# Norms of three tiles gathered in the tail, one sum moved to GpSimd, mixing by pairs, banks turned

## The reference

```python
zxbcdt = u @ in_proj_w.T                       # 512 -> 2 * 1024 + 2 * 128 + 64
z, xBC, dt_raw = jnp.split(zxbcdt, ...)
xBC = silu(causal_conv(xBC, 4 taps) + conv_b)
x, B, C = jnp.split(xBC, ...)
dt = softplus(dt_raw + dt_bias); A = -exp(A_log)
# in chunks of 64 tokens, 64 heads of 16 channels:
Y_diag = einsum(C, B, exp(differences of cumsum(dt * A)), x * dt)
state  = state * exp(sum(dt * A)) + einsum(B, decay to the chunk's end, x * dt)
Y_off  = einsum(C, state before the chunk, exp(cumsum(dt * A)))
y  = Y_diag + Y_off + x * D
yg = y * silu(z)
out = (yg * rsqrt(mean(yg ** 2) + eps) * norm_weight) @ out_proj_w.T
x1 = layernorm(u + out)
h  = silu(x1 @ w_gate.T) * (x1 @ w_up.T);  v = h @ w_down.T
result = layernorm(x1 + v / sqrt(mean(v ** 2) + eps))
```

## Time and profile before

| | us |
|---|---|
| median of 3 runs | 1842.28 |
| lowest and highest | 1840.56, 1845.46 |
| profiled execution, its own time | 1848.83 |
| span of the profiled execution | 1847.0 |
| PE busy | 1653.4 (90%) |
| DVE busy | 1382.8 (75%) |
| POOL busy | 1001.1 (54%) |
| ACT busy | 933.0 (51%) |

### The profile page before, as it was taken

How to read it: one execution, slowest core, us unless ns; L and a number is a source line. 1 busy time by engine, 2 the same in 40 slices (tenths; PEclk the granted TensorE clock), 3 DMA queues, 4 the chain that set the end, 5 groups by cost and what they waited for, 6 DMA issues and landing times. The chain is left out here.

```text
span 1847.0 us, 36975 instructions
## 1 busy us (share of the span) xinstructions
PE 1653.4 (90%) x11168; PEld 830.2 (45%) x11168; DVE 1382.8 (75%) x2200; ACT 933.0 (51%) x1647; POOL 1001.1 (54%) x1031
## 2 busy tenths in 40 slices
PE   2698999989989889888998898787999999999998
PEld 1244445444544444444544454454344444444443
DVE  6849858958867976985895896784777777777775
ACT  3454264444535335436444443432866666666662
POOL 0036526626625643652662663583877776767773
PEclk9899999999999999999999999898999999999999
DMA  6111131132124014113113212822001111101011
GB/s 220 50 39 28 49 86 49 28 79 69 29 54 102 16 55 104 28 49 83 51 30 75 72 29 54 228 47 62 35 23 47 57 35 47 57 35 52 29 35 58
DMA packets 214679, 109.66 MB, mean 59 GB/s; under 512 B 133796, under 2 KB 185696, under 8 KB 214496
## 3 DMA queue, kind: packets, MB, share of 16 engines
q1 hardware_dynamic: 214496, 107.37, 21.7%
HBM read 80.57 MB, written 26.76 MB: 58 GB/s over the span
## 5 line engine op out<-in xcount | busy, mean ns | idle before, releaser
L772 PE MATMUL ps_in<-u_hi,w_hi 128*128 128x512 f16 (+1 forms) x608 | 240.4, 395 | 80.4 <-DVE u_lo L1259 32.3
L1077 ACT ACTIVATE decay<-ps_d 128x512 f32<-128x512 f32 x256 | 149.8, 592 | 273.4 <-PE ps_d L830 222.3
L794 PE MATMUL ps_in<-w_out,zg 128*128 128x512 f32 x512 | 245.8, 636 | 32.9 <-DVE pre L1272 32.9
L1359 DVE TENSOR_TENSOR mix<-decay,gb 128x512 f32<-128x512 f32 x256 | 238.3, 938 | 47.7 <-issue 14.0
L1665 POOL TENSOR_TENSOR xend<-xpad,decay 128x256 f32<-128x256 f32 x256 | 186.9, 748 | 125.5 <-PE ps_yo L865 89.4
L772 PE MATMUL ps_in<-u_lo,w_hi 128*128 128x512 f16 (+1 forms) x608 | 238.6, 392 | 0.0
L772 PE MATMUL ps_in<-u_hi,w_lo 128*128 128x512 f16 (+1 forms) x608 | 237.6, 391 | 0.0
L1272 DVE SCALAR_TENSOR_TENSOR pre<-ps_in,cws,pre 128x511 f32<-128x511 f32 (+2 forms) x240 | 179.0, 746 | 34.1 <-ACT pre L1016 28.3
L1758 POOL TENSOR_TENSOR gate_sum<-gate_sum,gate_part 128x512 f32<-128x512 f32 x88 | 142.3, 1617 | 102.5 <-DVE gate_part L1586 102.3
L794 PEld LDWEIGHTS ps_in<-w_out,zg 128*128 128x128 f32 x512 | 101.2, 203 | 174.2 <-issue 172.3
L1016 ACT ACTIVATE pre<-ps_in,cb,cws 128x512 f32<-128x512 f32 x80 | 62.3, 779 | 181.2 <-PE ps_in L772 181.1
(11 more groups left out here) (181 smaller groups left out, 3743.3 us busy)
## 6 DMA issues: line engine op xcount, KB each, us to landing
ebc<-e_dram SPq DMA_DIRECT2D x256, 64.0 KB, 2.6
u<-u_t SPq DMA_DIRECT2D x9, 1024.0 KB, 5.0
res<-u_tok SPq DMA_DIRECT2D x32, 256.0 KB, 2.7
x_dram<-res SPq DMA_DIRECT2D x32, 256.0 KB, 2.0
xa<-x_dram SPq DMA_DIRECT2D x8, 1024.0 KB, 5.7
xr<-x_dram SPq DMA_DIRECT2D x32, 256.0 KB, 2.6
out<-xr SPq DMA_DIRECT2D x32, 256.0 KB, 2.0
fw_words<-gu_words SPq DMA_DIRECT2D x32, 176.0 KB, 3.1
```

Source lines behind the costliest of these rows:

```text
L772: last = mm(ps_in[bk][0:m, :], w[:, k, col:col + m], u[:, k, :], start=(k == 0 and j == 0), stop=(k == KT - 1 and j == 2))
L794: last = mm(ps_in[bk][:, :], zg[:, k, tt * P:(tt + 1) * P], w_out[:, k, :], start=(k == 0), stop=(k == CT - 1))
L1077: ac(decay[:, n % NG, :, :].rearrange("p a b -> p (a b)"), ps_d[n % 2][:, :], ACT.Exp).then_inc(e_done, 1)
L1359: v.tensor_tensor(mix[:, n % NG, :, :], decay[:, n % NG, :, :], gb[:, c % 2, 0:CH].unsqueeze(1).broadcast_to([P, CT, CH]), ALU.mult).then_ ...
```

## The change

- `banks_of` turns the two banks round behind q2: from x6 on, every use has the bank that it did not have before. x6 has the bank of q2, x7 that of o2, and so on.
- `res`, `bn`, `mv`, `rstd` and the semaphores `res_in` and `x1_out` have four places, one for each tile, where they had two. SyncE loads all four tiles of the residual at the start of a stage and stores all four at its end.
- `norm_tile` is split: `take_out` (forming `res`, which frees the bank) stays three slots after the projection; the statistics and the scaling of tiles 0 to 2 go to the tail, ahead of tile 3. GpSimd's second roots go with them, behind `sum_squares` of the last chunk and ahead of `root` of tile 3.
- The addition of `yoff` to `y` goes from VectorE (`y_before`) to GpSimd (`add_before`), at g = 3, ahead of `sum_squares`.
- `mixing` covers two slots with one instruction of 1024 columns, issued at every odd slot for the two slots that follow; `m_done` counts pairs.

```diff
 def banks_of(uses):
-    return [i % 2 for i in range(len(uses))]
+    names = [name for _, name in uses]
+    turned = names.index("q2") + 1 if "q2" in names else len(uses)
+    return [(i + (i >= turned)) % 2 for i in range(len(uses))]
...
-        res = sb("res", [P, 2, DM])
+        res = sb("res", [P, TT, DM])
...
             def body(st):
                 b = st.scan
-                load_res(b, 0)
-                load_res(b, 1)
+                for tt in range(TT):
+                    load_res(b, tt)
...
-                    for tt in range(2):
-                        if f"o{tt}" in st.at(n - NORM_END - 1):
-                            store_x1(b, tt)
-                            load_res(b, tt + 2)
-                store_x1(b, 2)
-                store_x1(b, 3)
+                for tt in range(TT):
+                    store_x1(b, tt)
...
             def within(b, n):
                 c, g = n // NG, n % NG
-                pe.wait_ge(m_done, b * SLOTS + n + 1)
+                pe.wait_ge(m_done, b * (SLOTS // 2) + n // 2 + 1)
...
             def exp_group(b, n):
                 act.wait_ge(d_full, b * SLOTS + n + 1)
-                need(act, m_done, b * SLOTS + n - 3)
+                need(act, m_done, b * (SLOTS // 2) + n // 2 - 1)
...
             def mixing(b, n):
-                dve.wait_ge(e_done, b * SLOTS + n + 1)
-                if n % NG == 0:
+                c, g = n // NG, n % NG
+                dve.wait_ge(e_done, b * SLOTS + n + 2)
+                if g == 0:
                     dve.wait_ge(t_free, (b * NC + c) * NA + 2)
-                need(dve, yd_done, b * SLOTS + n - 3)
-                v.tensor_tensor(mix[:, n % NG, :, :], decay[:, n % NG, :, :],
-                                gb[:, c % 2, 0:CH].unsqueeze(1).broadcast_to([P, CT, CH]), ALU.mult).then_inc(m_done, 1)
+                need(dve, yd_done, b * SLOTS + n - 2)
+                v.tensor_tensor(mix[:, g:g + 2, :, :].rearrange("p g e t -> p (g e) t"),
+                                decay[:, g:g + 2, :, :].rearrange("p g e t -> p (g e) t"),
+                                gb[:, c % 2, 0:CH].unsqueeze(1).broadcast_to([P, 2 * CT, CH]), ALU.mult).then_inc(m_done, 1)
...
             def y_before(b, c):
...
-                    dve.wait_ge(y1_done, b * 7 + c)
-                    dve.wait_ge(xd_done, b * NC + c + 1)
-                    v.tensor_tensor(y[:, c % 2, :, :], y[:, c % 2, :, :], yoff[:, :, :], ALU.add).then_inc(y2_done, 1)
...
-                    if n + 2 < SLOTS:
-                        mixing(b, n + 2)
+                    if n % 2 == 1 and n + 1 < SLOTS:
+                        mixing(b, n + 1)
...
                         if f"o{tt}" in st.at(n - NORM_AT):
-                            norm_tile(st, tt)
-                        if f"o{tt}" in st.at(n - NORM_END):
-                            norm_tile_end(st, tt)
+                            take_out(st, tt)
...
                 use_in(st, SLOTS, "x")
-                norm_tile_end(st, TT - 2)
+                for tt in range(TT - 1):
+                    norm_tile(st, tt)
+                for tt in range(TT - 1):
+                    norm_tile_end(st, tt)
                 use_in(st, SLOTS, "o")
...
+            def add_before(b, c):
+                pool.wait_ge(y1_done, b * 7 + c)
+                pool.wait_ge(xd_done, b * NC + c + 1)
+                g_.tensor_tensor(y[:, c % 2, :, :], y[:, c % 2, :, :], yoff[:, :, :], ALU.add).then_inc(y2_done, 1)
...
                     if g == 3 and c > 0:
+                        add_before(b, c)
                         sum_squares(b, c - 1)
...
-                        if f"o{tt}" in st.at(n - NORM_AT - 1):
-                            ln_root(b, tt)
                 gate(st, NC - 1)
-                ln_root(b, TT - 2)
                 sum_squares(b, NC - 1)
+                for tt in range(TT - 1):
+                    ln_root(b, tt)
                 root(st, TT - 1)
                 ln_root(b, TT - 1)
```

More of the change, by code:

```diff
@@ L65 @@
 SPLIT_SLOT = {1: (0, 1), 2: (2, 3)}
-NORM_AT, NORM_END = 3, 9
+NORM_AT = 3
 DEC = 352
@@ L285, in build @@
         rinv = sb("rinv", [P, TT])
-        bn = sb("bn", [P, 2, 6])
-        mv = sb("mv", [P, 2, 2])
-        rstd = sb("rstd", [P, 2])
+        bn = sb("bn", [P, TT, 6])
+        mv = sb("mv", [P, TT, 2])
+        rstd = sb("rstd", [P, TT])
         wmax = sb("wmax", [P, 2 * KT])
@@ L366, in build @@
         u_in = sem("u_in")
-        res_in = [sem("res_in0"), sem("res_in1")]
+        res_in = [sem(f"res_in{tt}") for tt in range(TT)]
         rq_in = [sem("rq_in0"), sem("rq_in1")]
@@ L374, in build @@
         parts_out = sem("parts_out")
-        x1_out = [sem("x1_out0"), sem("x1_out1")]
+        x1_out = [sem(f"x1_out{tt}") for tt in range(TT)]
         fw_in = [sem("fw_in0"), sem("fw_in1")]
@@ L559, in load_res @@
             def load_res(b, tt):
-                need(sp, x1_out[tt % 2], b * 32 + 16 * (tt // 2))
+                need(sp, x1_out[tt], b * 16)
                 settled(sp)
-                sp.dma_start(res[:, tt % 2, :], u_tok[bass.ds(b * L + tt * P, P), :]).then_inc(res_in[tt % 2], 16)
+                sp.dma_start(res[:, tt, :], u_tok[bass.ds(b * L + tt * P, P), :]).then_inc(res_in[tt], 16)
             def store_x1(b, tt):
@@ L567, in store_x1 @@
                 settled(sp)
-                sp.dma_start(x1_dram[bass.ds(b * L + tt * P, P), :], res[:, tt % 2, :]).then_inc(x1_out[tt % 2], 16)
+                sp.dma_start(x1_dram[bass.ds(b * L + tt * P, P), :], res[:, tt, :]).then_inc(x1_out[tt], 16)
             def load_fw(b, k):
@@ L648, in ahead @@
                 if n == 2 + W_STEPS:
-                    for k in range(2):
-                        sp.wait_ge(x1_out[k], 32)
+                    for tt in range(TT):
+                        sp.wait_ge(x1_out[tt], 16)
                     load_xa(0)
@@ L718, in _ @@
             body(Stage("last", nb - 1))
-            for k in range(2):
-                sp.wait_ge(x1_out[k], nb * 32)
+            for tt in range(TT):
+                sp.wait_ge(x1_out[tt], nb * 16)
             def load_xr(f, tt):
@@ L1060, in aux @@
                 else:
-                    need(act, m_done, b * SLOTS + NG * (c - 1))
+                    need(act, m_done, b * (SLOTS // 2) + 2 * (c - 1))
                     need(act, s_full, b * 14 + 2 * max(c - 1, 0))
@@ L1216, in ffn @@
                         if p.first and m == 1:
-                            for k in range(2):
-                                act.wait_ge(x1_out[k], nb * 32)
+                            for tt in range(TT):
+                                act.wait_ge(x1_out[tt], nb * 16)
                         silu(p, m)
@@ L1405, in mean_square, with take_out, norm_tile @@
                 v.tensor_scalar(msv[:, tt:tt + 1], src[:, 0:1], 1.0 / DI, 1e-5, ALU.mult, ALU.add).then_inc(free, 1)
-            def norm_tile(st, tt):
+            def take_out(st, tt):
                 b = st.scan
                 bk, _, full = st.bank(f"o{tt}")
-                i = tt % 2
-                ch = Chain(dve, ln_chain, 12, b)
-                ch.k = 3 * tt
                 dve.wait_ge(in_full[bk], full)
                 dve.wait_ge(rinv_done, b * TT + tt + 1)
-                dve.wait_ge(res_in[i], b * 32 + 16 * (tt // 2) + 16)
-                v.scalar_tensor_tensor(res[:, i, :], ps_in[bk][:, :], rinv[:, tt:tt + 1], res[:, i, :],
+                dve.wait_ge(res_in[tt], b * 16 + 16)
+                v.scalar_tensor_tensor(res[:, tt, :], ps_in[bk][:, :], rinv[:, tt:tt + 1], res[:, tt, :],
                                        ALU.mult, ALU.add).then_inc(in_free[bk], 1)
+            def norm_tile(st, tt):
+                bk, _, full = st.bank(f"o{tt}")
+                ch = Chain(dve, ln_chain, 12, st.scan)
+                ch.k = 3 * tt
                 dve.wait_ge(in_free[bk], full)
-                ch.step(v.bn_stats(bn[:, i, :], res[:, i, :]), settled)
-                ch.step(v.bn_aggr(mv[:, i, :], bn[:, i, :]))
-                v.tensor_scalar(mv[:, i, 1:2], mv[:, i, 1:2], 1e-5, None, ALU.add).then_inc(ln_chain, 1)
+                ch.step(v.bn_stats(bn[:, tt, :], res[:, tt, :]), settled)
+                ch.step(v.bn_aggr(mv[:, tt, :], bn[:, tt, :]))
+                v.tensor_scalar(mv[:, tt, 1:2], mv[:, tt, 1:2], 1e-5, None, ALU.add).then_inc(ln_chain, 1)
             def norm_tile_end(st, tt):
-                b, i = st.scan, tt % 2
-                dve.wait_ge(rstd_done, b * TT + tt + 1)
-                v.tensor_scalar(res[:, i, :], res[:, i, :], mv[:, i, 0:1], rstd[:, i:i + 1],
+                dve.wait_ge(rstd_done, st.scan * TT + tt + 1)
+                v.tensor_scalar(res[:, tt, :], res[:, tt, :], mv[:, tt, 0:1], rstd[:, tt:tt + 1],
                                 ALU.subtract, ALU.mult).then_inc(x1_done, 1)
@@ L1451, in body @@
                 mixing(b, 0)
-                mixing(b, 1)
                 for n in range(SLOTS):
@@ L1710, in ln_root @@
```

(2 more changed lines are left out.)

3 lines of the change are left out of this document (2 added, 1 removed).

## The result

The changed kernel takes 1782.78 us (median of 4 runs, 1782.3 to 1782.92). The kernel before, run beside it, took 1842.61 (median of 4 runs). The ratio is 0.9665, with a 95% interval of 0.9652 to 0.9679: about 60 us less. The profiled execution has a span of 1781.1 us where the one of before had 1847.0, a difference of 65.9. The forecast was 1767, 75 less, its range 1748 to 1808. Medians and ratios leave out executions in a second, slower state; among all kernels there was one, of 4176.86 us.

A forecast was written before the change was run, and what follows sets the result against it. TensorE was taken to bound the kernel: 10.0 us saved per body stage, 70 for seven, plus 5 in the last stage take the profiled 1848.8 to 1773.8, so the median becomes 1767 us, range 1748 to 1808.

The forecast's parts named there:

- The sum of a body stage: Terms for TensorE's idle time and granted clock in one body stage add up to 10.0 us less, 70 for seven.
- x6: First projection of the tail: with banks turned it no longer waits for `res`; net 2.8 us less per body stage.
- Rival B: Hollow turn: tail projection starts early, but idle time moves to later projections; 4 us a stage lost, 1795; chance 0.12.
- o0: First output projection of a body stage: its 1.92 us wait shrinks by 0.65, as a collision with `state_d` eats the rest.
- o1 and o2: Second and third output projections: less VectorE work ahead of them takes 2.8 and 0.9 us from their waits.
- Clock: Slow TensorE stretches after waits at o1 (seven stages) and x6 (five) return to full clock: 2.85 us per body stage.
- Mixing pairs: On VectorE, 32 instructions of 0.69 us become 16 of about 1.2: 1 to 3 us less per stage.
- rival A: GpSimd's sums collide with VectorE's two-operand instructions over shared SBUF ports, so gains shrink to 4.8 us a stage: 1808; chance 0.18.
- Norms in the tail: 5.2 us of VectorE norms and scalings move into 6.88 us of idle time ahead of q3's `msv`, at no cost.
- C: Slower: GpSimd's queue becomes the bound, `y_all` passing its delay to TensorE; decides at 1.4 us per chunk; 1895 at 2.5; chance 0.06.
- DMA queue: Four residual loads open a stage instead of two: 1.7 us more issue, slack remains, so no effect on body stages.
- Last stage: Stage without projections: smaller waits at `xt_lo`, `y` and elsewhere, less 1 for weight-row loads and less collisions: 5 us gained.

The follow-up runs named there:

- old counts: Changed kernel with each mixing pair counted as two on its semaphore, so waits on the mix read as before the change; 1766.95 us, ratio 0.9572.
- the length restored: Changed kernel with pairs counted as two, plus 15 redundant, always fulfilled waits in ScalarE's loop body (245 instructions); 1779.36 us, ratio 0.9638.

## Why the prediction was right, and where it was not

The kernels' profiles, split into TensorE's busy time (the matmuls are the same, so a difference is the clock) and the rest of the span. The last column is the stage shown above; in some kernels the stages differ by several us.

| kernel | span | PE busy | rest | a body stage |
|---|---|---|---|---|
| before | 1847.0 | 1653.4 | 193.6 | 150.2 |
| banks turned alone | 1819.6 | 1640.0 | 179.6 | 146.4 |
| sum on GpSimd alone | 1818.7 | 1650.3 | 168.4 | 146.8 |
| pairs alone | 1837.9 | 1658.4 | 179.5 | 150.2 |
| norms in the tail alone | 1814.3 | 1636.1 | 178.2 | 146.4 |
| changed kernel | 1781.1 | 1626.2 | 154.9 | 142.8 |
| changed, old counts | 1771.4 | 1629.4 | 142.0 | 139.5 |
| the same, sum on VectorE | 1802.6 | 1638.9 | 163.7 | 146.9 |

The profiled execution with the old counts took 6.3 us more than the median of its runs, and its last stage is 5.5 us longer than the changed kernel's; its row shows less gain than the median does.

- **The sum of a body stage** was 10.0 us, 7.15 of idle time and 2.85 of clock. With the wait at the jump taken away (old counts) the stage lost 10.7: 7.4 of idle time and 3.3 of clock. The parts alone gave 3.8, 3.4, 0 and 3.8 a stage, 11.0 together. That the two totals agree does not show that the parts are independent: with the sum back on VectorE the other three gave 3.3 and not 7.6, so the sum was worth 7.4 there and 3.4 alone.
- **x6**: forecast 2.8 net, measured 3.1 at x6 and 0.2 at z0. `msv` was done at once and x6 began 0.05 us after it, as laid out. Rival B (hollow turn) does not hold: the turn alone kept 3.8 us in the stage shown and 4.3 in the mean of the seven. But it came another way than laid out: 1.7 of idle time and 2.5 of clock, where 2.8 of idle time and 1.1 of clock were expected. What B names, idle time that moves elsewhere, is seen in two stages only, ahead of x4 and at `from_before` and not at z0 or o3 (0.4 there), and it is absent in the stage whose o1 ran at 0.58. So it goes with o1's full clock and not with the turn.
- **o0**: 0.65 forecast, 1.57 measured. The step that failed is the collision of the pair with `state_d`. That instruction now ends at 710.45, 0.4 us after the pair's start, and the pair took 1.50 us for 1.22:

```profile
710.03 1.50 DVE L1358 TENSOR_TENSOR mix<-decay,gb 128x1024 f32<-128x1024 f32 x1
```

  It lost 0.3, not the 0.6 to 0.75 that was taken off. The gain lies even above the 1.4 that was counted without any collision; where the last 0.2 come from is not shown.
- **o1 and o2**: both waits are gone, as forecast. Two others are in their place that were not forecast, 0.75 at a new state ahead of x4 and 0.45 at x4 itself, which takes o1's bank and needs its `res` formed.
- **Clock**: 2.85 forecast, 3.2 measured. The term was taken too small by a misreading: the slow stretch at x6 is in all seven body stages of the kernel before (granted clock 0.66, 0.54 and five times 0.52 or 0.53), not in five, and 1.7 + 1.6 is 3.3. The mechanism was told too simply, too. It was bound to the length of the waits at o1 and x6; in the run with the norms alone o1's wait stayed at 1.76 and its slow stretch went together with the wait ahead of it, and with the banks turned alone equal waits at o1 left 0.58 in one stage and 1.00 in another. The price of a stretch can be read from its row, the condition for it cannot be read from the waits next to it.
- **Mixing pairs**: the estimate of 1.2 us was right (1.22 median, 2.91 at most; 1.40 in the mean, below the 1.6 that was to speak for rival A). Alone they shorten the first and the seventh stage by some 3 us; in the five between, the 1.2 us of idle time that they save go back to the clock.
- **Norms in the tail** cost nothing, as said. The idle time ahead of q3's `msv` fell from 6.88 us to

```profile
797.74 0.16 DVE L1402 TENSOR_SCALAR msv<-ps_yo 128x1 f32<-128x1 f32 x1 [2.44 <-PE ps_yo L780]
```

  so 4.4 of the cover are used.
- **Rivals A and C.** `y_all` does wait for GpSimd's add, against what was said of it:

```profile
L1392 DVE TENSOR_TENSOR y<-ps_yd,y x64: 675/691/692, 120.9 to 1199.8; 128x512 f32<-128x512 f32 x64
its engine sat idle before it (us, times) until:
  POOL y L1685: 34.2, 26
who waited for it (us, times):
  PE ps_yd L840: 1.3, 1
```

  1.3 us in each of 26 chunks of 56, near the 1.4 at which C was to begin. But TensorE waited for `y` once. The step that was too strict in C is that `y_all`'s delay is handed on whole: VectorE had that much time before the state additions were due (TensorE waited for `state` twice, 0.9 us in all). Collisions are rare (the add takes 1.26 us at the median and 2.25 at most), and the sum alone gave its 3.4 a stage. The rule of the Trainium skill (SBUF — State Buffer, Who interferes with whom) is not contradicted: the pair above met GpSimd. Its price there was 0.3 us, and for the 128 pairs, mean less median, 0.18 each. The prediction gave the rule without the exception that the section makes for the 2-port perf modes, and found the trace in full agreement. The earlier trace rows has a row that does not fit the rule as it was given: the scaling of `res` reads one SBUF tensor only and takes 0.54 us at the median, but 1.26 at 792.07, where GpSimd's skip term runs beside it. Which mode it ran in is not shown.
- **DMA queue: "Nothing for the body stages."** The loads cost nothing, as shown with four buffers alone. What is missing from the prediction is another step altogether: of the change it costed the work on each engine and never the code. The five jumps took 12 to 20 us (old counts against the changed kernel 16; with the length restored 12).
- **Last stage**: 5 forecast, 5.5 measured.

In the span the forecast was 9 us too far: some 20 from the jumps, less about 10 from o0, x6, z0, the clock, the prologue and the last stage, which were each taken a little low or not at all. So the 9 us are two larger errors of opposite sign. The median missed by 15.8, 6.7 more. The profiled execution of before had lain 6.5 above the median of its runs, and this was taken off as if it would be so again; the profiled execution of after took 1782.91 us, 0.1 above its median.

## What to carry to other kernels

A change that moves no work can lengthen an engine's program: waits against a loop variable cost register operations, and counts that need new multiples cost more of them. Compare the length of each engine's loop body and the packets of the instruction queue before and after, and look at the head of a loop for an engine that idles on "issue". An "each part alone" series is worth its runs: here the parts alone added up to the whole, and yet with one of them missing the loss was twice what that part had given alone. Take such a part out of the finished kernel as well before its gain is named. And look at every stage: the same waits can stand at either level of the clock.

## What the hardware showed that was not expected

- A step at the loop's jump: ScalarE idle for 0 us with a loop body of 223 to 231 instructions, counted without semaphores, 3 to 4 us with 245, 247 and 276, and 79 to 86 packets on the instruction queue against 104 or 105. In each of the 20 waits one packet of 8 KB of that queue starts while ScalarE stands.
- The granted clock behind one and the same wait: 0.58 after 1.09 + 1.92 us at o1 in the kernel before, 1.00 after 1.76 alone in the kernel with the norms in the tail, and with the banks turned alone, after waits of 1.08 and 1.83, 1.00 in two stages and 0.50 to 0.63 in four. It is so within the kernel before as well: behind o0, after 0.22 and 1.92 us, 0.60 (452.60 to 456.60) and 1.00 (755.00 to 759.00). What tells one case from the other was not found.
